# Second matmul of a mixture of experts: weights stationary, tokens moving, float32r parts in place of float32

## The reference

```python
def _L3_ffn_ref(x, gate_w, gate_b, w1, b1, w2, b2):
    scores = jnp.einsum('bsd,de->bse', x, gate_w) + gate_b
    probs = jax.nn.softmax(scores, axis=-1)
    topk_vals, topk_idx = jax.lax.top_k(probs, TOP_K)
    mask = jnp.sum(jax.nn.one_hot(topk_idx, NUM_EXPERTS, dtype=probs.dtype), axis=-2)
    masked = probs * mask
    masked = masked / (jnp.sum(masked, axis=-1, keepdims=True) + 1e-09)
    h = jax.nn.gelu(jnp.einsum('bsd,edh->ebsh', x, w1) + b1[:, None, None, :], approximate=False)
    y = jnp.einsum('ebsh,ehd->ebsd', h, w2) + b2[:, None, None, :]
    out = jnp.einsum('bse,ebsd->bsd', masked, y)
    return out
...
t = t + _L3_ffn_ref(_ln_t(t), ...)
```

## Time and profile before

| | us |
|---|---|
| median of 3 runs | 1001.02 (998.97 to 1004.37) |
| span of the profiled execution | 1000.7 |
| of it: last attention loop ends, last write of `tok` | 802.7 |
| layernorm, transposes, gate logits | 802.7 to 835.6 |
| eight blocks of experts on PE | 836.6 to 990.8 |
| last block on DVE, store | 990.9 to 1000.7 |

### The profile page before, as it was taken

One profiled execution on the slowest core, in us unless ns is written; L12 is line 12 of the kernel. 1 busy time (PEld: TensorE's weight loads), 2 busy tenths in 40 slices (PEclk: granted clock), 3 DMA queues, 4 the chain that ended last, 5 costly groups with the idle time before them and its releaser, 6 DMA issues.

```text
span 1000.7 us, 19812 instructions
## 1 busy us (share of the span) xinstructions
PE 826.8 (83%) x5997; PEld 667.3 (67%) x5997; DVE 733.6 (73%) x2103; ACT 586.7 (59%) x1826; POOL 138.3 (14%) x200
## 2 busy tenths in 40 slices
PE   0875799999999466999997776489999949999996
PEld 0761566666666364778885456278788738999995
DVE  6317799999999653899998599479999972354344
ACT  0211678777777224888887652378889842444442
POOL 9002333333333000000000000000000010000000
PEclk9997899999999776999999797679999967999998
DMA  5000000000000643566664000246666600000000
GB/s 187 1 0 1 1 0 0 0 0 0 0 0 0 57 70 48 90 85 94 94 94 63 1 0 1 32 78 85 91 94 94 91 4 1 9 8 16 8 8 16
DMA packets 51260, 38.05 MB, mean 38 GB/s; under 512 B 28448, under 2 KB 43296, under 8 KB 50976
## 3 DMA queue, kind: packets, MB, share of 16 engines
q1 hardware_dynamic: 50784, 36.14, 23.8%
q0 software_dynamic: 448, 1.57, 0.6%
HBM read 6.24 MB, written 3.15 MB: 9 GB/s over the span
## 4 chain that ended last, share of the span: by engine, by line
PE 65%; DVE 22%; issue 5%; DMA 4%; SPq 2%; ACT 2%; DVEq 0%; ACTq 0%
PE ps L660 9%; PE ps L790 8%; PE ps L610 8%; PE ps L769 7%; PE ps L557 6%; PE ps L564 6%; DVE sqj L995 3%; PE ps L601 3%; PE ps L566 3%; DVE ee L958 2%; PE ps L574 2%; PE ps L575 2%; DVE on L856 2%; DVE chst L837 2%; DVE xn L831 2%
## 5 line engine op out<-in xcount | busy, mean ns | idle before, releaser
L380 ACT ACTIVATE ee<-ps,nmax 128x128 f32<-128x128 f32 (+1 forms) x588 | 248.9, 442 | 10.2 <-DVE nmax L917 7.7
L958 DVE TENSOR_SCALAR ee<-ee,rrec 128x128 f32<-128x128 f32 (+1 forms) x588 | 173.4, 358 | 5.2
L660 PE MATMUL ps<-w,ee 128*128 128x128 f32 x960 | 137.3, 280 | 19.7 <-DVE ee L958 19.7
L367 ACT ACTIVATE big<-ps 128x384 f32<-128x384 f32 (+1 forms) x224 | 113.3, 538 | 40.4 <-PE ps L660 39.5
L660 PEld LDWEIGHTS ps<-w,ee 128*128 128x128 f32 x960 | 104.2, 142 | 45.3 <-DVE ee L958 33.7
L380 ACT ACTIVATION_READ_ACCUMULATOR ee<-ps,nmax 128x1 f32 x588 | 124.1, 211 | 0.0
L917 DVE TENSOR_REDUCE nmax<-ps 128x2 f32<-128x256 f32 x200 | 101.1, 546 | 18.1 <-PE ps L566 18.1
L564 PE MATMUL ps<-qk 128*128 128x128 f32 (+1 forms) x400 | 103.8, 349 | 12.6 <-DMA qk<-lo 9.6
L471 ACT ACTIVATE big<-ps 128x512 f32<-128x512 f32 x96 | 57.3, 597 | 84.5 <-PE ps L769 83.2
L790 PEld LDWEIGHTS ps<-w,big 128*128 128x128 f32 x768 | 98.1, 191 | 7.1
L564 PEld LDWEIGHTS ps<-qk 128*128 128x128 f32 x400 | 79.9, 207 | 30.6 <-issue 17.1
(11 more groups left out here) (215 smaller groups left out, 1296.4 us busy)
## 6 DMA issues: line engine op xcount, KB each, us to landing
qk<-hi SPq DMA_DIRECT2D x36, 192.0 KB, 3.7
qk<-hi SPq DMA_DIRECT2D x72, 96.0 KB, 3.8
qk<-lo SPq DMA_DIRECT2D x36, 192.0 KB, 4.8
qk<-lo SPq DMA_DIRECT2D x72, 96.0 KB, 4.6
w<-w_in SPq DMA_DIRECT2D x1, 1829.5 KB, 13.9
xc<-x_in SPq DMA_DIRECT2D x4, 384.0 KB, 5.9
l_mix<-on SPq DMA_DIRECT2D x8, 192.0 KB, 6.5
tok<-l_mix POOLq DMA_DIRECT2D x4, 384.0 KB, 4.9
```

Of the source, the lines that this page charges most:

```text
L367: nc.scalar.activation(et[:, h, 0:w], ps[:, 4 + hh, 0:w], ACT.Copy).then_inc(own(l, f"et{hh}"), 1)
L380: last = nc.scalar.activation(ee[:, ke, hh, qc, 0:w], src, ACT.Exp, bias=nmax[:, kp, hh, qc:qc + 1], accum_out=rsum[:, kp, hh, qc:qc + 1])
L660: last = nc.tensor.transpose(ps[:, 4 + hh, b * P:(b + 1) * P], ee[:, u, hh, qc, tc * P:(tc + 1) * P], ident)
L958: last = V.tensor_scalar(v, v, rrec[:, kp, hh, qc:qc + 1], None, ALU.mult)
```

## The change

1. **Second matmul.** For each hidden piece PE now issues three float32r matmuls with the weights `w2` stationary (128x96) and 512 tokens moving: w2 high x h high, w2 low x h high, w2 high x h low (`expert_out`). The result has channels on partitions, one PSUM bank for each expert. They come three pieces behind `hidden` (`LAG = 3`).
2. **Splitting the gelu output.** ACT writes the gelu to `hf` (four buffers, in `ee`). POOL copies it to float32r (the high part), DVE subtracts that from it (the low part): one instruction of 128x512 on each for every piece, in four buffers `hhl`. ACT waits for the low part of four pieces earlier, POOL for PE's use of that buffer.
3. **Gating and sum.** For each expert of a block DVE does (y + b2) x gate in one instruction of 96x512 (`gate_expert`), and POOL adds it to `xc`, the residual with channels on partitions (`add_expert`). The bias add, product, sum and residual add of before are gone. SP stores `xc`; the output is channel-major.
4. **Gate by DMA.** The gate is written expert-major, PE transposes it (128x128), DVE copies it to SBUF, SP stores it in DRAM, and for each block loads it back spread over 96 partitions (768 KB, two buffers). PE waits for the gate and its copy between the third and the fourth hidden piece.
5. **Residual to channels.** Ahead of the layernorm's transposes PE transposes the 32 tiles of `tok`, and ACT copies them into `xc`, eight copies of 96x512, ahead of the square root in ACT's order.
6. **Gate logits** of a group stand between the transposes of the next groups instead of after all of them. The splitting of `xn` moves from DVE to POOL. `w2` is split on POOL at the start of the third attention loop.
7. Small: the loops over blocks are unrolled; the first block's one-step semaphores are merged into three; `b2` moves from the 128-row weights to the 96-row weights.

```diff
+        w2hl = nc.alloc_sbuf_tensor_at("w2hl", [P, 2, NS * C], F32R, offset=big_at)
+        hhl = nc.alloc_sbuf_tensor_at("hhl", [P, 4, 2, 512], F32R, offset=big_at + 2304 * 4)
...
+            sp.wait_ge(sg("moe_gate_t"), 1)
+            sp.dma_start(gate_d.rearrange("e (t k) -> (e t) k", k=P), gate_t).then_inc(sg("moe_gate_stored"), 16)
+            sp.wait_ge(sg("moe_gate_stored"), 16)
+            load_gates(0)
+            load_gates(1)
...
+            for n in range(NS * NB):
+                t, s = n // NS, n % NS
+                if s == 0 and 1 <= t < NB - 1:
+                    split(t + 1)
+                pool.wait_ge(sg("moe_h"), n + 1)
+                if n >= 4:
+                    pool.wait_ge(sg("moe_y"), n - 3)
+                nc.gpsimd.tensor_copy(hhl[:, n % 4, 0, :], hf[:, n % 4, :]).then_inc(sg("moe_hi"), 1)
+                if n >= 8 and (n - 8) % NJ == 0:
+                    add_expert((n - 8) // NJ)
...
-            with act.Fori(0, NT // 4) as t:
-                for s in range(NE * NJ):
-                    act.wait_ge(sg("moe_h_ps"), t * (NE * NJ) + (s + 1))
-                    nc.scalar.activation(h3[:, s % 4, :], ps[:, 4 + s % 4, :], ACT.Gelu).then_inc(sg("moe_h"), 1)
+            for n in range(NS * NB):
+                act.wait_ge(sg("moe_h_ps"), n + 1)
+                if n >= 4:
+                    act.wait_ge(sg("moe_lo"), n - 3)
+                nc.scalar.activation(hf[:, n % 4, :], ps[:, 4 + n % 4, :], ACT.Gelu).then_inc(sg("moe_h"), 1)
...
-                            for q in range(4):
-                                if r == 0:
-                                    pe.wait_ge(sg("moe_y"), t * 4 + (q + 1))
-                                last = mm(ps[:, q, e * C:(e + 1) * C], h3[:, r % 4, q * P:(q + 1) * P],
-                                          wb("f3_w2")[:, r * C:(r + 1) * C], start=(j == 0), stop=(j == NJ - 1))
...
+                pe.wait_ge(sg("moe_hi"), n + 1)
+                pe.wait_ge(sg("moe_lo"), n + 1)
+                if j == 0 and t >= 1:
+                    pe.wait_ge(sg("moe_gated"), NE * (t - 1) + e + 1)
+                for k, (w, h) in enumerate(((0, 0), (1, 0), (0, 1))):
+                    last = mm(ps[0:C, e, :], w2hl[:, w, s * C:(s + 1) * C], hhl[:, n % 4, h, :],
+                              start=(j == 0 and k == 0), stop=(j == NJ - 1 and k == 2))
+                last.then_inc(sg("moe_y"), 1)
...
+            for n in range(LAG):
+                hidden(n)
+            pe.wait_ge(sg("f3_gate"), 1)
+            nc.tensor.transpose(ps[:, 0, P:2 * P], gate[:, 0, :, :].rearrange("p t e -> p (t e)"), ident).then_inc(sg("moe_gate_ps"), 1)
+            pe.wait_ge(sg("moe_gate_t"), 1)
+            for n in range(LAG, NS * NB):
+                hidden(n)
+                expert_out(n - LAG)
...
+            for n in range(NS * NB):
+                dve.wait_ge(sg("moe_hi"), n + 1)
+                V.tensor_tensor(hhl[:, n % 4, 1, :], hf[:, n % 4, :], hhl[:, n % 4, 0, :].bitcast(F32), ALU.subtract).then_inc(sg("moe_lo"), 1)
+                if n == 0:
+                    dve.wait_ge(sg("moe_gate_ps"), 1)
+                    V.tensor_copy(gate_t, ps[:, 0, P:2 * P]).then_inc(sg("moe_gate_t"), 1)
+                if n >= 6 and (n - 6) % NJ == 0:
+                    gate_expert((n - 6) // NJ)
```

More of the change, by code:

```diff
@@ L117, in hybrid_kernel @@
         big = sb("big", [P, NJ * NG * GT])
+        big_at = nc.sbuf_base - NJ * NG * GT * 4
         ones = sb("ones", [P, P])
@@ L464, in _ @@
                             nc.scalar.activation(y1[:, :, g * GT:(g + 1) * GT], y1[:, :, g * GT:(g + 1) * GT], ACT.Gelu).then_inc(sg("f2_gelu"), 1)
+            for g in range(8):
+                act.wait_ge(sg("xres_ps"), g + 1)
+                nc.scalar.activation(xc[:, g * 512:(g + 1) * 512], ps[0:C, g % 4, :], ACT.Copy).then_inc(sg("xres"), 1)
             norm_tail("lnf3")
@@ L496, in normed_to_channels @@
                     last.then_inc(sg("ln_t_ps"), 1)
+                    if after is not None and g >= 1:
+                        after(g - 1)
+                if after is not None:
+                    after(7)
             pe.wait_ge(sg("w128_loaded"), 16)
@@ L773, in _ @@
[L773 to L792 removed]
+            for g in range(8):
+                if g >= 4:
+                    pe.wait_ge(sg("xres"), g - 3)
+                for t in range(4):
+                    last = nc.tensor.transpose(ps[0:C, g % 4, t * P:(t + 1) * P], tok[:, g * 4 + t, :], ident)
+                last.then_inc(sg("xres_ps"), 1)
@@ new lines, in gate_logits, with hidden @@
+            def gate_logits(g):
+                pe.wait_ge(sg("xn_copied"), TURN["lnf3"] + g + 1)
+                for t in range(4 * g, 4 * g + 4):
+                    last = mm(ps[:, 0, t * NE:(t + 1) * NE], xn[:, t * P:(t + 1) * P], wa("f3_gate"), start=True, stop=True)
+                last.then_inc(sg("f3_gl_ps"), 1)
+            pe.wait_ge(sg("xres"), 8)
+            normed_to_channels("lnf3", gate_logits)
+            def hidden(n):
+                t, s = n // NS, n % NS
+                if s == 0:
+                    pe.wait_ge(sg("moe_x"), t + 1)
+                if n >= 4:
+                    pe.wait_ge(sg("moe_h"), n - 3)
+                for k, (w, x) in enumerate(((0, 0), (0, 1), (1, 0))):
+                    last = mm(ps[:, 4 + n % 4, :], w1hl[:, w, s * P:(s + 1) * P], xhl[:, t % 2, x, :], start=(k == 0), stop=(k == 2))
+                last.then_inc(sg("moe_h_ps"), 1)
@@ new lines, in _ @@
+            LAG = 3
+            pe.wait_ge(sg("f3_wlo"), 1)
+            pe.wait_ge(sg("f3_w2lo"), 1)
+            for n in range(LAG):
[6 more added lines that the diff above has]
+                expert_out(n - LAG)
+            for n in range(NS * NB - LAG, NS * NB):
+                expert_out(n)
@@ new lines, in _, with gate_expert @@
+            by_expert = gl.rearrange("p t e -> p (t e)").rearrange("p (e t) -> p t e", e=NE)
+            V.tensor_tensor(by_expert, ge, last_dim(st[:, 1, :], NE), ALU.mult).then_inc(sg("f3_gate"), 1)
+            def gate_expert(k):
+                t, e = k // NE, k % NE
+                dve.wait_ge(sg("moe_y"), NJ * (k + 1))
+                if e == 0:
+                    dve.wait_ge(sg(f"moe_gates{t % 2}"), 16 * (t // 2 + 1))
+                if k >= 2:
+                    dve.wait_ge(sg("moe_sum"), k - 1)
+                V.scalar_tensor_tensor(out=ytmp[:, k % 2, :], in0=ps[0:C, e, :], scalar=wa("f3_b2", C)[:, e:e + 1], in1=gates[:, t % 2, e, :],
+                                       op0=ALU.add, op1=ALU.mult).then_inc(sg("moe_gated"), 1)
@@ L1164 @@
+            for k in range((NS * NB - 7) // NJ + 1, NE * NB):
+                gate_expert(k)
 def kernel(**inputs):
@@ L1218 @@
         "f2_b2": rows(get("L2_ffn_b2")),
-        "f3_w2": get("L3_ffn_w2").reshape(NE * NJ, P, C).transpose(1, 0, 2).reshape(P, -1), "f3_b2": rows(get("L3_ffn_b2")),
+        "f3_w2": get("L3_ffn_w2").reshape(NE * NJ, P, C).transpose(1, 0, 2).reshape(P, -1),
     }
```

200 lines of the change are left out of this document (94 added, 106 removed).

## The result

The changed kernel takes 1015.04 us, median of four runs (1013.15 to 1016.55), against 1001.01 for the kernel before: ratio 1.0132, 95% interval 1.0107 to 1.0156. It is slower by 14 us (1.3%). 985.4 was forecast, with a range of 971 to 1004. The third rival came in by its sign and its size, and the rows show its exclusion of nearly whole instructions too; its sum for the step, though, is not what sets the step.

What follows compares the result with a forecast made beforehand. POOL, slowed beside DVE to 1.47 us a step, was taken to bound the loop: PE's release at 840.2 + 94.5 steps (138.9) + 1.5 start-up + 4.5 tail = 985.1, given as 985.4 us; range 971 to 1004.

Steps and rivals of the forecast that it cites:

- The third rival: Expert loop: POOL and DVE exclude each other for whole instructions, 1.67 to 1.86 us a step, 1004 to 1022 us; chance 0.13.
- POOL then sets the pace: Expert loop: POOL's 1.47 us a step, just above PE's 1.40, was taken as the step.
- The size of the exclusion: Expert loop: POOL and DVE shutting each other out at SBUF adds 0.38 us to POOL's step, from 0.27 to 0.50.
- POOL busy over 90%: Expert loop: sign expected in the profile, with POOL's copies longer than 0.66 us.
- One addition of POOL in that time still fits: Expert loop: a piece's gelu, copy and subtraction take 2.3 of PE's 4 us, leaving room for one POOL addition.
- no bound: Expert loop: DVE needs 0.92 us a step plus 0.12 to 0.41 of waiting, 1.3 at most, so it does not limit.
- the start-up term of 1.5 us: Start of the expert loop: PE's full clock returns some 4 us into dense work, adding 1.5 us.
- The second: Rival, expert loop: POOL gives most of the gain back, step 1.56 to 1.67 us, 994 to 1004 us; chance 0.15.
- The first: Rival, expert loop: POOL is no bound, PE's 1.40 us a step holds and the clock stays up, 969.8 us; chance 0.10.
- partial blocking: POOL beside DVE: in the earlier trace's 4.45 us batch, DVE's 2.50 us beside it cost POOL only 0.99 us.
- PE's floor: Expert loop: a hidden piece and its output cost PE 1.40 us a step, 0.18 less than before.
- The straight line from 256 to 1536 columns: POOL's instructions at 512 columns, interpolated between traced sizes: copy 0.66 us, two-input operation 1.10 us.

Runs made afterwards that it cites:

- the kernel with the later addition: Changed kernel with POOL's addition of each expert placed two pieces later in its order; 1001.45 us, ratio 0.9982 against the kernel before.
- narrow addition: Changed kernel with POOL adding only 16 of the 512 columns, the sum left out for the others; 979.68 us, ratio 0.9785 against the kernel before.
- the kernel with the PSUM read: Changed kernel with DVE's subtraction reading the hidden piece's PSUM bank (value ahead of the gelu) instead of SBUF; 983.1 us, ratio 0.9819 against the kernel before.
- the relieved kernel: Changed kernel with ACT computing the gelu twice (high part, then exactly, in PSUM) and no POOL copies; 977.5 us, ratio 0.9752 against the kernel before.
- the kernel with the gate off the path: The relieved kernel with the gate's transpose behind the fifth hidden piece and all products three pieces later; 976.42 us, ratio 0.974 against the kernel before.
- the kernel with both edits: Changed kernel with the subtraction reading PSUM and POOL's addition two pieces later; 980.05 us, ratio 0.9778 against the kernel before.

## Why the prediction was wrong, point by point

| | forecast | measured |
|---|---|---|
| PE a step, where nothing holds it | 1.40 | 1.37 to 1.40 |
| POOL busy a step, alone | 1.04 to 1.17 | 1.10 |
| POOL busy a step, beside DVE | 1.47 | 1.40 |
| DVE busy a step | 1.04 to 1.33 | 1.31 |
| step | 1.47 | 1.79 |
| last write of `tok` to PE's release | 37.5 | 37.4 |
| behind the last output | 4.5 | 4.9 |

**The step that failed** is "POOL then sets the pace", the equation of the step with POOL's busy time. The size of the exclusion, on which the prediction spent its care, came out near: 0.30 us a step on POOL's busy time where 0.38 had been put in, so that this busy time is 1.40 and not 1.47. The sign that the prediction named for it, POOL busy over 90%, failed: it is busy 78% of the loop. What the prediction left out is the 0.39 us a step in which POOL, the fullest engine behind PE, waits: 24.2 of 37 us for DVE's product, which stands behind a subtraction that POOL itself has held up; the kernel with the later addition, in which this wait is 1.3 us, takes 1.63 a step.

Part of the rest is the splitting of `xn`, which the prediction spread over twelve steps and which comes at once: without one in them, the same kernel's steps take 1.41. "One addition of POOL in that time still fits" and DVE as "no bound" were each true of averages; in the queues an addition of 1.67 us, at times with a splitting behind it, meets copies that DVE and PE want at once.

The step is off by 0.39 - 0.07 = 0.32, and 0.32 x 94.5 = 30 us, more than the whole error of the end, which was due at 985.1 and came at 1011.2: 4.5 us of it go, since the loop began 3.0 us earlier (837.23 in place of 840.2) and the measured step contains the start-up term of 1.5 us. Part of the 30 is the clock, which dips behind such waits (below), 5 us at most.

**The rivals.** The third forecast 1.67 to 1.86 us a step and a time of 1004 to 1022; both held. That the exclusion covers nearly whole instructions was right too. Its arithmetic, however, took POOL's busy time with the exclusion for the step, and that grew to 1.40 only; the runs with the later and with the narrow addition come in below the full sum. So its time is right in part by luck. The second would have been what the later addition gives (1.63, 1001 us). The first is what comes when the exclusion or the copies are gone.

**Partial or full.** The rows show that an addition and a subtraction hold each other up, in both directions, for about their whole length: 2.32 in place of 0.69, and 2.32 in place of 1.29. The Trainium skill, in SBUF — State Buffer, section Who interferes with whom, calls contention for the port pair that the two engines share an exclusive lock, and names a DVE instruction with two SBUF inputs beside a GpSimd instruction that reads SBUF as a case of it. These rows agree but for the 0.14 us at each handing over, and they agree with its exception of an instruction with at most one SBUF input: the product stays at 734 to 747 ns. The prediction read the partial stretching in the earlier trace rows as partial blocking.

**PE's floor** was right: 1.37 us in the undisturbed steps, 1.401 to 1.407 over whole loops with their slow start.

**POOL's instructions.** The copy of 512 columns takes 0.61 us (0.66 forecast), the addition 1.26 to 1.29 (1.10). The straight line from 256 to 1536 columns missed the second by a sixth. The two errors nearly cancel, together with the fact that only six splittings fall in the loop: in the kernel with the PSUM read POOL's durations add up to 107.4 us, 1.14 a step (1.17 forecast), and they overlap each other by 0.04 (0.08 was taken).

**Ahead of the loop.** Timeline:

```profile
799.77 1.47 POOL L334 CAST qk<-w 128x1536 fp32r<-128x1536 f32 x1 [13.83 <-DMA qk<-lo]
...
800.58 4.00 ACT L528 ACTIVATE xc<-ps 96x512 f32<-96x512 f32 x8 [2.37 <-PE ps L829]
801.32 2.90 POOL L336 TENSOR_TENSOR qk<-w,qk 128x1536 fp32r<-128x1536 f32 x1
804.59 1.28 ACT L388 ACT_TABLE_LOAD   x1
...
807.52 0.23 ACT L388 ACTIVATE st<-st 128x32 f32<-128x32 f32 x1 [1.65 <-DVE st L930]
...
809.31 1.91 PE L560 MATMUL ps<-w,on 128*96 128x128 f32 x8 [5.72 <-ACT on L397]
...
825.77 3.41 PE L835 MATMUL ps<-w,xn 128*128 128x4 f32 x16
...
829.05 4.19 PE L848 MATMUL ps<-qk 128*128 128x512 f32 x9
```

The residual's copies cost nothing, as forecast: ACT still waited 1.65 us for DVE, and the square root came 7.7 us behind the last write of `tok` (799.8), as before. That this write came at 799.8 and not at 802.7 is no effect of the change: in kernels that are the same up to there it lay between 797.5 and 804.4. So the splitting of `w2` leaves no mark, but the traces could not show 3 us either. Logits and transposes take 2.43 us a group (2.29 forecast) and 19.7 in all (18.3): the logits of a group 1.57 (1.33), its transposes 0.86 (0.96). The 1.33 came from the count of a 2 us window, which includes instructions that reach over its edges. They began 2.8 us sooner behind `tok` than before, though, because POOL's long subtraction (`L336`) ran at once and not in the middle of DVE's normalising; no step had that. Why it had waited there ("issue") is open.

**The gate.** Timeline:

```profile
832.14 1.40 DVE L1206 TENSOR_TENSOR gsel<-cmp 128x32 f32<-128x32 f32 x4
832.23 1.17 POOL L374 CAST hhl<-ee 128x512 fp32r<-128x512 f32 x2 [17.27 <-ACT ee L536]
...
836.38 0.47 PE L869 MATMUL ps<-w,gate 128*128 128x128 f32 x1 [3.14 <-DVE gate L1219]
...
837.23 1.65 PE L848 MATMUL ps<-qk 128*128 128x512 f32 x3 [0.38 <-DVE ee L1237]
```

The forecast had PE's release 7.2 us behind the first hidden piece, it was 8.2. DVE's chain took 7.1 us in place of 5.8 (5.9 in the relieved kernel), since its small two-input instructions met POOL's first copies: `L1206` 1.40 us, against 0.48 in the kernel with the gate off the path, which has no such copies. This and the longer logits cancel the earlier start: 37.4 us from `tok` to release, 37.5 forecast. That total is right by compensation. The gate's loads (768 KB) took 6.8 us and were in time.

## What to carry to other kernels

An engine's busy time a step is a floor for the step, not its price: where two engines below 85% hand work to each other in both directions, follow one period through both in-order queues, with the longest instruction of each in the worst place, before taking the fuller one's busy time. Where a late instruction waits for another engine's result, put it far enough behind (here two pieces, 14 us for free). Work that comes once a block counts where it stands, not only in the average. Let DVE's two-input work beside POOL read one operand from PSUM, or take work off POOL; the kernel with ACT writing the high part does both and keeps the result. Stretched instructions were harmless here as long as both queues had slack in front of the bound.

## What the runs showed of the hardware

- A DVE subtraction with two SBUF inputs and a POOL copy or addition shut each other out in SBUF for all but 0.12 to 0.16 us: the one held up ends that much before the other's end plus its own time alone, in each of the 142 stretched subtractions and in 181 of the 189 stretched POOL instructions of three loops. The other eight, copies of 0.9 to 1.0 us, end before any subtraction beside them; why they are longer is open. With one input in PSUM nothing is stretched (subtraction 673 to 693 ns, addition 1257 to 1303).
- Having come first does not secure the next place: in 17 of the 50 cases in the changed kernel a second POOL instruction ran ahead of the waiting subtraction, as the copy at 849.29 did. In the other 33 it ran behind the first one. What decides it is open.
- PE's granted clock falls behind its waits in the loop. Windows of the changed kernel:

```profile
902.00:904.00 2.00, 1.74 (x5) 1.29 (x6) 2.00 (x4) 0.00 (x0) 1.73 (x2) 0.59 0.00 0
904.00:906.00 2.00, 2.00 (x7) 1.43 (x6) 0.28 (x2) 0.60 (x1) 2.00 (x3) 0.55 0.00 0
```

They follow a wait of 1.85 us for POOL that ends at 902.26. PE waits so long (1.84 to 2.13 us) once in each of six blocks; behind three of the waits the clock falls to 1.2 GHz, behind the other three it stays at 2.4, and what tells them apart is open. Besides its first 4 us, some 10 us of the loop stand at the lower level (each window's share worked out from its granted clock), which costs 5 us at most. In the kernel with both edits and in the relieved one no window between 846 us and the last output is below 1.00.
- ACT writes a gelu of 128x512 from PSUM to float32r in SBUF in 0.598 us and in place in PSUM in 0.582, and to plain float32 in SBUF the changed kernel's takes 0.598 as well (`L536`), so the rounding costs nothing. PE does not wait for ACT even when it does both.
